# Expert weights copied block by block into a ring by ScalarE, so that TensorE's matmuls have fixed addresses

## What is computed

```python
logits = jnp.einsum('bsd,de->bse', x, gate_w) + gate_b
probs = jax.nn.softmax(logits, axis=-1)
top_probs, top_idx = jax.lax.top_k(probs, 2)
top_probs = top_probs / jnp.sum(top_probs, axis=-1, keepdims=True)
...
h1 = jnp.einsum('bsd,edh->bseh', x, w1)
h2 = jnp.einsum('bsd,edh->bseh', x, w2)
hidden = jax.nn.silu(h1) * h2
expert_out = jnp.einsum('bseh,eho->bseo', hidden, w3)
return jnp.einsum('bseo,bse->bso', expert_out, dispatch)
```

## Time and profile before

| what | value |
| --- | --- |
| median of 3 executions | 589.88 us |
| the profiled execution, its own time | 589.5 us |
| its span (first to last instruction) | 587.7 us |
| PE / PEld busy | 214.6 / 174.4 us |
| DVE / ACT / POOL busy | 163.5 / 105.8 / 287.6 us |
| mean granted TensorE clock | 0.623 of full |

### The profile page before, as it was taken

How to read it: one execution, slowest core, us unless ns; L and a number is a source line. 1 busy time by engine, 2 the same in 40 slices (tenths; PEclk the granted TensorE clock), 3 DMA queues, 4 the chain that set the end, 5 groups by cost and what they waited for, 6 DMA issues and landing times.

```text
span 587.7 us, 5198 instructions
## 1 busy us (share of the span) xinstructions
PE 214.6 (37%) x1607; PEld 174.4 (30%) x1608; DVE 163.5 (28%) x281; ACT 105.8 (18%) x172; POOL 287.6 (49%) x293
## 2 busy tenths in 40 slices
PE   5586693020000311001799841010178795000000
PEld 5364682000000310000787740000077684000000
DVE  4945678982000000000233300000024435011011
ACT  5746562100000100000332210000033231000000
POOL 1480237477777777774000067777400001777772
PEclk9777655555555555555699965555567996555555
DMA  8990000000000600000011161111000112111111
GB/s 297 248 397 9 1 1 0 11 23 27 25 27 25 204 29 25 27 27 18 19 52 41 69 205 26 27 27 27 17 19 37 37 55 92 43 45 27 43 45 30
DMA packets 20940, 35.26 MB, mean 60 GB/s; under 512 B 5788, under 2 KB 6172, under 8 KB 20276
## 3 DMA queue, kind: packets, MB, share of 16 engines
q1 hardware_dynamic: 12468, 26.51, 13.3%
q0 software_dynamic: 8288, 8.41, 6.0%
q10 hardware_dynamic: 160, 0.01, 0.0%
HBM read 18.13 MB, written 16.78 MB: 59 GB/s over the span
## 4 chain that ended last, share of the span: by engine, by line
issue 42%; PE 26%; DVE 16%; POOL 11%; ACT 3%; DMA 1%; another core or an unknown queue 1%; POOLq 0%; ACTq 0%; DVEq 0%
POOL scratch L985 10%; PE banks L671 7%; PE banks L661 5%; PE banks L662 5%; PE banks L645 2%; PE banks L528 1%; DVE ct L726 1%; PE banks L561 1%; PE banks L548 1%; PE banks L503 1%; DVE pwc L766 1%; DVE ssq L729 1%; DVE m L832 1%; DVE top L832 1%
## 5 line engine op out<-in xcount | busy, mean ns | idle before, releaser
L980 POOL DMA_INDIRECT sorted_x<-shared,place x128 | 125.0, 977 | 49.7 <-issue 38.7
L905 DVE SCALAR_TENSOR_TENSOR power<-banks,fold 128x512 f32<-128x512 f32 x40 | 27.5, 691 | 304.0 <-remote 178.6
L985 POOL DMA_INDIRECT scratch<-sorted_y,place x64 | 61.3, 958 | 97.6 <-DMA sorted_y<-enh 78.4
L985 POOL DMA_INDIRECT xs<-sorted_y,place x64 | 60.5, 946 | 85.0 <-DMA sorted_y<-filt 65.8
L661 PE MATMUL banks<-shared,w_hi 128*128 128x128 f16 x320 | 63.5, 243 | 51.0 <-issue 50.9
L662 PE MATMUL banks<-shared,w_lo 128*128 128x128 f16 x320 | 63.9, 241 | 48.6 <-issue 47.4
L671 PE MATMUL banks<-w_all,power 128*128 x320 | 50.6, 301 | 41.4 <-issue 40.6
L671 PEld LDWEIGHTS banks<-w_all,power 128*128 128x128 f32 x320 | 46.9, 219 | 45.2 <-issue 45.2
L456 ACT COPY shared<-banks 128x1024 f16<-128x1024 f16 x20 | 20.2, 1012 | 206.3 <-PE banks L645 106.6
L661 PEld LDWEIGHTS banks<-shared,w_hi 128*128 x320 | 35.6, 111 | 58.2 <-issue 54.2
L662 PEld LDWEIGHTS banks<-shared,w_lo 128*128 x320 | 34.6, 108 | 56.1 <-issue 54.0
(11 more groups left out here) (144 smaller groups left out, 337.1 us busy)
## 6 DMA issues: line engine op xcount, KB each, us to landing
sorted_x<-zeros SPq DMA_DIRECT2D x2, 2560.0 KB, 29.7
w_raw<-sorted_x SPq DMA_DIRECT2D x20, 256.0 KB, 2.9
w_raw<-in_L_ffn_w SPq DMA_DIRECT2D x5, 512.0 KB, 16.1
sorted_y<-filt SPq DMA_DIRECT2D x10, 256.0 KB, 2.0
sorted_y<-enh SPq DMA_DIRECT2D x10, 256.0 KB, 2.0
xs<-in_x SPq DMA_DIRECT2D x8, 256.0 KB, 5.1
sorted_x<-shared,place POOLq DMA_INDIRECT x128
out<-cen_sq SPq DMA_DIRECT2D x8, 256.0 KB
```

The source lines that it names most:

```text
L905: nc.vector.scalar_tensor_tensor(hid[:, q % RING, :], bank[2 + q % 2], HSCALE / WSCALE, gated[:, q % 2, :], ALU.mult, ALU.mult).then_inc(h ...
L980: nc.gpsimd.indirect_dma_start(out=sorted_x[k], out_offset=bass.IndirectOffsetOnAxis(ap=place[:, k, j, t:t + 1], axis=0), in_=parts[:, HT ...
L985: nc.gpsimd.indirect_dma_start(out=yg[k][:, j, t, :], out_offset=None, in_=sorted_y[k], in_offset=bass.IndirectOffsetOnAxis(ap=place[:, k, ...
```

## The change

ScalarE takes over the choice of the expert. The five weight parts of an expert (w1 high and low, w2 high and low, w3) now lie next to each other in one array `w_all`, 640 elements of 16 bits for each partition and expert. For each block ScalarE copies these 640 elements into a ring `fetched_w` of 4 quads (16 blocks), which takes the room of arrays that are no longer needed; `fetch(q)` makes the 4 copies of a quad. The owners are loaded into ScalarE's registers, once per octet. TensorE reads the ring at fixed addresses and has no register instruction in the expert part; it waits for a new semaphore `fetched` instead. `fetch(0)` and `fetch(1)` run as soon as the owners are known; afterwards `fetch(q + 2)` stands behind `gate(q)` in ScalarE's list, and from quad 4 on it waits for `y_ps`, that is for the matmuls of `down(q - 4)` to be done with the ring's place.

```diff
+        w_all = sb("w_all", [P, E, EXPERT], U16)
+        w1_hi, w1_lo, w2_hi, w2_lo = (w_all[:, :, a * HID:(a + 1) * HID].bitcast(F16) for a in range(4))
+        w3_all = w_all[:, :, 4 * HID:].bitcast(F32)
...
+        work = sb("work", [P, 5, 2 * BLK])
+        pw, pwc, mag, gain = (work[:, a, :].rearrange("p (k n) -> p k n", k=2) for a in range(4))
+        fold2 = work[:, 4, :].rearrange("p (c n) -> p c n", c=4)
+        fetched_w = work[:, :, :].rearrange("p a n -> p (a n)").bitcast(U16).rearrange("p (r n) -> p r n", n=EXPERT)
...
+            regs = [[nc.scalar.alloc_register(f"owner{s}_{b}") for b in range(OCT)] for s in range(2)]
+            experts = {}
+
+            def fetch(q):
+                n = q // 2
+                if q % 2 == 0:
+                    nc.scalar.load(regs[n % 2], owner[0:1, n // OCTETS, n % OCTETS * OCT:(n % OCTETS + 1) * OCT])
+                    experts[n] = [nc.scalar.snap(r, min_val=0, max_val=E - 1) for r in regs[n % 2]]
+                if q >= RING:
+                    act.wait_ge(y_ps, q - RING + 1)
+                for b in range(QUAD):
+                    last = nc.scalar.copy(fetched_w[:, (q % RING) * QUAD + b, :],
+                                            w_all[:, bass.ds(experts[n][(q % 2) * QUAD + b], 1), :].rearrange("p o n -> p (o n)"))
+                last.then_inc(fetched, 1)
...
+            act.wait_ge(owner_done, HALVES)
+            act.wait_ge(wsplit, 3)
+            for q in range(FETCH_AHEAD):
+                fetch(q)
...
                     gate(q)
+                    if q + FETCH_AHEAD < HALVES * NQ:
+                        fetch(q + FETCH_AHEAD)
...
-            def of_expert(w, e):
-                return w[:, bass.ds(e, 1), :].rearrange("p o n -> p (o n)")
-
-            def up(q, experts):
+            def weights_of(q, b, a, width):
+
+                return fetched_w[:, (q % RING) * QUAD + b, a * HID:a * HID + width]
+
+            def up(q):
                 n = q // 2
                 if q % 2 == 0:
                     pe.wait_ge(xt_done, n + 1)
-                for hi, lo, first_bank, out_done, in_use in ((w1_hi, w1_lo, 0, h1_done, silu_done), (w2_hi, w2_lo, 2, h2_done, hid_done)):
+                pe.wait_ge(fetched, q + 1)
+                for a, first_bank, out_done, in_use in ((0, 0, h1_done, silu_done), (2, 2, h2_done, hid_done)):
...
-                        nc.tensor.matmul(dst, of_expert(hi, experts[s]), tokens, start=True, stop=False)
-                        last = nc.tensor.matmul(dst, of_expert(lo, experts[s]), tokens, start=False, stop=True)
+                        nc.tensor.matmul(dst, weights_of(q, b, a, HID).bitcast(F16), tokens, start=True, stop=False)
+                        last = nc.tensor.matmul(dst, weights_of(q, b, a + 1, HID).bitcast(F16), tokens, start=False, stop=True)
...
                     last = nc.tensor.matmul(bank[4 + q % 2][:, b * C:(b + 1) * C], hid[:, q % RING, b * P:(b + 1) * P],
-                                            of_expert(w3_all, experts[s]), start=True, stop=True)
+                                            weights_of(q, b, 4, 2 * C).bitcast(F32), start=True, stop=True)
```

More of the change, by code:

```diff
@@ L11 @@
 I32 = mybir.dt.int32
+U16 = mybir.dt.uint16
 ALU = mybir.AluOpType
@@ L41 @@
 SLOTS = SLOT_BLOCKS * P
+EXPERT = 4 * HID + 2 * C
+FETCH_AHEAD = 2
 OROWS = OCT * P
@@ L177, in build @@
         fold1 = sb("fold1", [P, 2, 2, QPIX])
-        fold2 = sb("fold2", [P, 4, QPIX])
         power = sb("power", [P, 2, 2, BLK])
-        pw = sb("pw", [P, 2, BLK])
+        work = sb("work", [P, 5, 2 * BLK])
+        pw, pwc, mag, gain = (work[:, a, :].rearrange("p (k n) -> p k n", k=2) for a in range(4))
+        fold2 = work[:, 4, :].rearrange("p (c n) -> p c n", c=4)
+        fetched_w = work[:, :, :].rearrange("p a n -> p (a n)").bitcast(U16).rearrange("p (r n) -> p r n", n=EXPERT)
         proj = pw[:, :, :].rearrange("p a (u r) -> p (a u) r", r=2 * M)
-        pwc = sb("pwc", [P, 2, BLK])
-        mag = sb("mag", [P, 2, BLK])
         rmag, passed, guard, small = (scratch[:, k, :, :] for k in range(4))
-        gain = sb("gain", [P, 2, BLK])
         filt = sb("filt", [P, 4, QPIX])
@@ L249, in build @@
         in_xg = [sem(f"in_xg{o}") for o in range(OCTETS)]
-        xt_ps, xt_done, h1_done, h2_done, silu_done, hid_done, y_ps, y_done = (
-            sem(n) for n in ("xt_ps", "xt_done", "h1_done", "h2_done", "silu_done", "hid_done", "y_ps", "y_done"))
+        xt_ps, xt_done, h1_done, h2_done, silu_done, hid_done, y_ps, y_done, fetched = (
+            sem(n) for n in ("xt_ps", "xt_done", "h1_done", "h2_done", "silu_done", "hid_done", "y_ps", "y_done", "fetched"))
         y_stored = [sem(f"y_stored{r}") for r in range(RING)]
@@ L261, in build @@
         ct_cen = ct[:, :, 0:P].rearrange("p u (h c) -> p u h c", h=2)
-        weight_parts = ((w1_raw[:, :, :], w1_hi[:, :, :], w1_lo[:, :, :]), (w2_raw, w2_hi[:, :, :], w2_lo[:, :, :]))
+        weight_parts = ((w1_raw, w1_hi, w1_lo), (w2_raw, w2_hi, w2_lo))
         def mean_cols(t):
@@ L409, in _ @@
                     act.wait_ge(in_w3, 16)
-                    nc.scalar.activation(w3_all[:, :, :], w3_raw, ACT.Copy, scale=WSCALE).then_inc(wsplit, 1)
+                    nc.scalar.activation(w3_all, w3_raw, ACT.Copy, scale=WSCALE).then_inc(wsplit, 1)
             load_table(ACT.Sqrt)
@@ L627, in _ @@
                 ranks(k)
-            regs = [[nc.tensor.alloc_register(f"owner{s}_{b}") for b in range(OCT)] for s in range(3)]
-            def owners(n):
-                k, o = n // OCTETS, n % OCTETS
-                if o == 0:
-                    pe.wait_ge(owner_done, k + 1)
-                nc.tensor.load(regs[n % 3], owner[0:1, k, o * OCT:(o + 1) * OCT])
-                return [nc.tensor.snap(r, min_val=0, max_val=E - 1) for r in regs[n % 3]]
             def transpose_tokens(n):
@@ L660, in up, with down @@
                         dst, tokens = bank[first_bank + q % 2][:, b * P:(b + 1) * P], xt[:, n % 2, s * P:(s + 1) * P]
-                        nc.tensor.matmul(dst, of_expert(hi, experts[s]), tokens, start=True, stop=False)
-                        last = nc.tensor.matmul(dst, of_expert(lo, experts[s]), tokens, start=False, stop=True)
+                        nc.tensor.matmul(dst, weights_of(q, b, a, HID).bitcast(F16), tokens, start=True, stop=False)
+                        last = nc.tensor.matmul(dst, weights_of(q, b, a + 1, HID).bitcast(F16), tokens, start=False, stop=True)
                     last.then_inc(out_done, 1)
-            def down(q, experts):
+            def down(q):
                 pe.wait_ge(hid_done, q + 1)
@@ L669, in down @@
                 for b in range(QUAD):
-                    s = (q % 2) * QUAD + b
                     last = nc.tensor.matmul(bank[4 + q % 2][:, b * C:(b + 1) * C], hid[:, q % RING, b * P:(b + 1) * P],
-                                            of_expert(w3_all, experts[s]), start=True, stop=True)
+                                            weights_of(q, b, 4, 2 * C).bitcast(F32), start=True, stop=True)
                 last.then_inc(y_ps, 1)
@@ L681, in transpose_sums @@
                 last.then_inc(out_ps, 1)
-            pe.wait_ge(wsplit, 3)
             pe.wait_ge(place_done, HALVES)
             for k in range(HALVES):
-                experts = {OCTETS * k: owners(OCTETS * k)}
                 transpose_tokens(OCTETS * k)
@@ L691, in _ @@
                     if i % 2 == 0 and i // 2 + 1 < OCTETS:
-                        experts[n + 1] = owners(n + 1)
                         transpose_tokens(n + 1)
                     if i < NQ:
-                        up(q, experts[n])
+                        up(q)
                     if i >= DOWN_LAG:
-                        down(q - DOWN_LAG, experts[(q - DOWN_LAG) // 2])
+                        down(q - DOWN_LAG)
                     if k and i in RESULT_AT:
```

3 lines of the change are left out of this document (removed).

## The result

| | kernel before | changed kernel |
| --- | --- | --- |
| median | 589.83 us (589.6 to 590.0, 4 runs) | 609.56 us (608.91 to 611.77, 4 runs) |
| profiled execution, its span | 589.5, 587.7 us | 610.09, 608.3 us |

The changed kernel is slower: ratio 1.0341, 95% interval 1.0314 to 1.0369. The forecast was 612, range 599 to 640.

A forecast was written before the change was run, and what follows sets the result against it. GpSimd was taken to set A and C, the expert part B and D, with TensorE the bound in B before and ScalarE after. 589.5 + 12.7 (B) + 9.2 (D) = 611.4 profiled, forecast 612 us, range 599 to 640.

The forecast's parts named there:

- The mechanism: Expert part: ScalarE becomes the bound through its new copies, making the kernel slower; chance 0.78, own range 598 to 638 us.
- step of a copy: ScalarE, start to start of one 640-element copy: 0.65 us, bounds 0.54 and 0.85.
- register load exposed in B and D: ScalarE's load of owners into registers, once per octet: 0.3 us not hidden, bounds 0 and 1.3.
- B: Expert stretch, 282.2 to 331.9 us before: silu 2 to silu 19 grows from 48.9 to 61.6 us, +12.7.
- D: Expert stretch, 429.7 to 485.2 us before: silu 22 to silu 39 grows from 55.5 to 64.7 us, +9.2.
- octet on ScalarE: Eight copies, two silus, a token copy and a register load: 7.4 us, against 6.23 for TensorE before.
- `fetch` waiting for `down`, costed at 0: ScalarE's fetch(q) waits for down(q - 4), a quad's time old by then: wait costed at 0.
- two results: In D, behind quads 7 and 13 of the half: ScalarE waits 2.5 us, copies 0.5; 6.0 for two.
- A and C: Slow stretches, 204.4 to 281.0 and 347.0 to 425.4 us, beside GpSimd's indirect DMAs: pace unchanged, cost 0.
- TensorE idle for a third: Sign expected in B and D: TensorE idle about a third, waiting for fetched or silu.
- The second rival: Registers make TensorE slow beside indirect DMAs in A and C; without them 459 us; chance 0.10.
- Quicker copies: Copies quicker than the rows say: no change around 0.48 us per copy, below it possibly 580 us; chance 0.06.

The follow-up runs named there:

- Run 11: Changed kernel with ScalarE's copies kept, but TensorE loads registers again and reads the stored weights; nobody reads the ring: 612.32 us, ratio 1.0378 to the kernel before.
- run 3: Changed kernel with fetch copying 320 of 640 elements from quad 4 on, output not right: 447.42 us, ratio 0.9944 to the kernel before, on chip 14.
- run 9: Changed kernel without copies; TensorE reads stored weights of fixed experts, output not right: 563.78 us, ratio 0.9557 to the kernel before.
- run 10: Changed kernel with all copies moved from ScalarE to VectorE, whole computation done: 571.15 us, ratio 0.9674 to the kernel before.
- run 5: Changed kernel measured again without an edit: 608.9 us, ratio 1.034 to the kernel before.
- run 6: Changed kernel with 60 register-free matmuls put ahead of the experts on TensorE, output unused: 616.44 us, ratio 1.0457 to the kernel before.
- run 2: Changed kernel with ScalarE's copies kept, TensorE's registers back and the ring unread, on chip 14: 462.74 us, ratio 1.0285 to the kernel before.
- Run 7: Kernel before, with GpSimd's scatters of half 1 held back until the experts of half 0 are done: 594.33 us, ratio 1.0082.
- run 8: Changed kernel with copies shared, blocks 0 and 1 of each quad on ScalarE, 2 and 3 on VectorE: 578.11 us, ratio 0.9813 to the kernel before.
- run 1: Changed kernel without copies, TensorE reading stored weights at fixed places, output not right, on chip 14: 448.28 us, ratio 0.9967 to the kernel before.

## Why the prediction was right, point by point

**The mechanism.** Run 11 shows that with ScalarE's copies alone the time is within 3.4 us of the changed kernel's, run 3 that the cost goes with the copies' elements, run 9 that the rest of the change is a gain, and run 10 that 18.1 of its 25.5 us remain when VectorE makes the same copies. So the result has two parts: the fixed addresses give 25.5 us (run 9), and the copies on ScalarE take 45 (run 5 less run 9, each beside a kernel before at 589.7 and 589.3). The gain disappears since it falls to an engine that has stopped being the bound: TensorE's octet could go to 4.27 us, ScalarE's stands at 6.87.

| term | predicted | measured |
| --- | --- | --- |
| step of a copy | 0.65 us | 0.623 |
| register load exposed in B and D | 0.3 us | 0 |
| octet on ScalarE | 7.4 us | 6.87 |
| silu 2 to silu 19 | 61.6 us | 61.2 |
| silu 22 to silu 39 | 64.7 us | 83.9 |
| B, by the first gather | +12.7 | +9.2 |
| D, by the second gather | +9.2 | +10.6 |
| end | 612 | 609.6 |

The mechanism was right. That the time came out within 2.4 us is in part luck: the copies and loads were put too high, the waits of `fetch` too low, and D's own stretch was cut at a silu that moved.

**The copy.** The cast's row and the slope per element gave 0.03 us too much, 3.6 us over 132 copies. The Trainium skill, page "ScalarE: Activation LUTs", section "What ACT_TABLE_LOAD costs", led to an estimate of 0.63, and the trace agrees: 0.623.

**The register load.** In B `fetch` starts 0.49 us behind the silu with a load as without one (290.31 to 290.80, 300.57 to 301.06), so nothing of it shows; 17 times 0.3 is 5.1 us of the sum. Outside B and D it shows twice: 0.28 us behind a single silu (203.86), and 0.20 us behind a token copy and a silu (354.19), both soon after ScalarE had been idle. The Trainium skill, page "Runtime: NRT & Kernel Launch", section "Instruction fetch mechanics", has about 200 ns per register; whether the load takes that long in itself no run here shows, only that it stays hidden where earlier copies are queued ahead of the 1.4 us of silu and token copy, and not quite where those 1.4 us stand alone.

**`fetch` waiting for `down`, costed at 0.** Here the sum was short, and errors cancelled. 17 fetches of 2.49 us, 17 silus and 7 token copies are 57.0 us; B took 61.2. So in B 4.6 us too much (1.9 for the copies, 2.7 for the loads) stood against 4.2 us of waits costed at nothing. 3.1 us of these are `fetch(4)`, which waits at 283.92 for the first `down`, still at the slow pace. In D the stretch that the prediction counted, from silu 22, is of no use: silu 22 came early (421.25, before 429.69), `fetch(24)` behind it waited 17.06 us, and 83.9 us passed where 64.7 were forecast. From silu 23 to silu 39, 63.8 us pass where it was 55.0 (430.18 to 485.21 before, the first silu of the pair at 429.69 plus 0.49): two results with waits of 2.43, as predicted to a tenth, but behind each result the `fetch` waits 1.25 and 1.99 us more. The prediction's own terms give 61.3 us for this stretch (64.7 less one `fetch` of 2.6, its load and a silu). And silu 23 comes 92.55 us after the first gather, where it was 90.56: 2.0 later. It stands behind `fetch(24)`, which could start at 438.91, when `down(20)` was through, and whose copies fill the time up to 441.41; the sum had no such term. That they make all of the 2.0 us was not isolated. 8.8 + 2.0, less 0.2 behind silu 39, is the 10.6.

**A and C at no cost.** The pace did not change; the start did. Silu 2 came at 280.19 and not at 282.93, so 12.3 us more in B (61.2 - 48.9) are 9.2 at the gather. But silu 2 is a poor mark for where B begins: in run 5 it came 5.1 us earlier still, and the gather 0.4 us. What counts is silu 3, behind `fetch(4)`, which waits for the slow pace to end. It came at 286.43, 3.0 us later than before (283.42, the first silu of the pair at 282.93 plus 0.49), and from there to silu 19 55.0 us pass where it was 48.4: 3.0 + 6.5, less 0.3 behind silu 19, is the 9.2.

**TensorE idle for a third.** In B it was busy for 49.14 of 61.00 us, idle for a fifth, and in D for 44.20 of 63.00, idle for three tenths. Its granted clock, the mean over stretches at the full and at the lower level, fell from 0.94 to 0.78 of full in B and from 0.86 to 0.74 in D, and passes at the lower level are longer (0.31 us at 322.06, 0.22 at 324.81). It still stayed ahead of ScalarE in the steady octets.

**The second rival,** registers as the cause of A and C, had 0.10 and 459 us. The changed kernel's own rows refute it, and run 6 does: register-free passes take 2.8 us. Its price was well worked out all the same: on the chip without the crawl, run 2 has ScalarE's copies as the pace of the experts and takes 462.7 us. Run 7 shows the other side: with registers and no indirect DMA beside them there is no crawl.

**Quicker copies.** Parity was put at 0.48 us per copy. Run 3, on the chip where GpSimd hid the gain, has the octet at 5.34 us with steps of 0.36, below TensorE's 6.23, and so agrees in direction; the point itself was not measured. Below it the wait for `down` comes in, which the prediction had at nothing.

## What to carry to other kernels

Before work is moved off the bounding engine, add up one period of the engine that takes it, from start-to-start steps of neighbouring rows: here 8 steps of 0.62 us on an engine that already had 1.9 us per octet made 6.9, above the 6.2 they were to relieve. Then try the same instructions on each engine that can run them; on VectorE they were 2.6 times as quick and the same idea won 3%. And where an engine copies into a ring, look at what stands behind a copy that waits for its place: silus 3 and 23 stood 2.5 us behind such copies, and halving the copies (runs 3 and 8) left octets of 5.34 and 5.16 us where 4.27 were possible.

## What I had not expected of the hardware

- **The slow pass is not there on every chip.** The kernel before took 449.8 us on chip 14, 589.7 and 589.3 on chip 15 at two times, and 589.8 beside the result. Beside indirect DMAs a pass took 2.8 us in the slow cases, and on chip 14 TensorE kept its full pace (run 1: 467 passes in 35.6 us). What differs was not found, nor whether it is the chip or its state at the time: chip 14 was used once.
- **Something gets through at full pace first.** Counted back from the time of silu 1 at 2.8 us per pass, 29 or 30 passes get through before the crawl in A of the kernel before, and some 35 to 38 in the kernels without registers: silu 1 comes at 233.19 and 239.26 us with registers in TensorE's list (before, run 11), and at 217.86, 213.39, 216.91, 211.16 and 215.17 without (changed, runs 5, 8, 9 and 10). With 60 passes put ahead (run 6) fewer of the experts' get through. It looks as if register instructions use up some of what gets through, though they do not change the pace; this is argued from the times of the signals alone.
- **A copy of 640 16-bit elements** takes a step of 0.24 us on VectorE and 0.62 on ScalarE, both with the expert's register in the address.
